# Gated cross-attention and ternary feed-forward block: half the roundings and most of the turns of a unit go from the gate-and-up stage to the down stage, and an input's rounding follows its scale at once

## The reference

```python
def h_bitlinear(x, w):                       # used for gate, up and down
    xq = act_quant(fwht(x))                  # Hadamard transform, then 8 bits per token
    wq = weight_quant(w)                     # ternary weights
    return jnp.einsum('bsh,oh->bso', xq, wq)

x = x + tanh(g_xattn) * attention(layernorm(x), ctx, ctx)        # 32 heads of 16, 8 key heads
gate = h_bitlinear(layernorm(x), w_gate)                         # 512 -> 2048
up   = h_bitlinear(layernorm(x), w_up)
x = x + tanh(g_ffn) * h_bitlinear(silu(gate) * up, w_down)       # 2048 -> 512
```

## Time and profile before

| | us |
|---|---|
| median of 3 runs (lowest, highest) | 530.8 (528.2, 534.39) |
| the profiled execution | 533.5 |
| its span, first to last instruction | 531.6 |

### The profile page before, as it was taken

One profiled execution on the slowest core, in us unless ns is written; L12 is line 12 of the kernel. 1 busy time (PEld: TensorE's weight loads), 2 busy tenths in 40 slices (PEclk: granted clock), 3 DMA queues, 4 the chain that ended last, 5 costly groups with the idle time before them and its releaser, 6 DMA issues.

```text
span 531.6 us, 9904 instructions
## 1 busy us (share of the span) xinstructions
PE 489.0 (92%) x3436; PEld 306.1 (58%) x3436; DVE 401.2 (75%) x772; ACT 320.8 (60%) x504; POOL 215.5 (41%) x313
## 2 busy tenths in 40 slices
PE   3899999989899999869989899989999999989997
PEld 2556666656555444357844458754448864479553
DVE  4768997887666449928988947988965988978791
ACT  3368886777677768757633527643446653388381
POOL 3226456797866441743006634203924200920000
PEclk9999999999899999969999999999999999999999
DMA  7997010010020040000000010000011000000012
GB/s 220 332 353 233 8 34 1 15 28 2 1 80 2 1 160 1 0 1 2 1 1 1 1 59 20 0 0 0 0 39 41 2 0 1 1 1 1 21 60 80
DMA packets 19705, 24.00 MB, mean 45 GB/s; under 512 B 1808, under 2 KB 14480, under 8 KB 19664
## 3 DMA queue, kind: packets, MB, share of 16 engines
q1 hardware_dynamic: 19248, 22.68, 13.4%
q10 hardware_dynamic: 416, 0.79, 0.4%
HBM read 19.26 MB, written 4.19 MB: 44 GB/s over the span
## 4 chain that ended last, share of the span: by engine, by line
PE 62%; issue 17%; DVE 13%; ACT 4%; POOL 2%; DMA 1%; POOLq 1%; SPq 1%; DVEq 0%; ACTq 0%
PE ps L752 9%; PE ps L834 9%; PE ps L535 9%; PE ps L518 7%; PE ps L784 6%; PE ps L561 5%; DVE wst L1345 3%; PE ps L578 3%; DVE wst L1340 2%; DVE reg L1181 2%; PE ps L543 2%; PE ps L681 2%; PE ps L608 2%; ACT y_split L1059 1%; DVE wst L1302 1%
## 5 line engine op out<-in xcount | busy, mean ns | idle before, releaser
L752 PE MATMUL ps<-wst 128*128 128x512 bf16 x512 | 114.2, 379 | 1.5 <-DVE su L1314 1.5
L1181 DVE TENSOR_REDUCE reg<-ps 128x4 f32<-128x512 f32 x128 | 82.0, 685 | 38.3 <-PE ps L535 37.1
L535 PE MATMUL ps<-reg 32*128 32x256 f32 x512 | 91.6, 447 | 1.6 <-DMA reg<-in_k_t 0.9
L488 POOL TENSOR_TENSOR reg_rest<-reg_rest,z_sc 128x1024 f32<-128x1024 f32 x24 | 51.4, 2175 | 90.1 <-DVE z_sc L1383 90.1
L903 ACT ACTIVATE reg<-ps 128x1024 f32<-128x1024 f32 x64 | 65.4, 1022 | 33.6 <-PE ps L543 30.3
L752 PEld LDWEIGHTS ps<-wst 128*128 128x128 bf16 x512 | 48.9, 98 | 58.3 <-DVE su L1314 1.8
L1039 ACT ACTIVATE wst<-wst 128x512 f32<-128x512 f32 x64 | 40.1, 629 | 67.6 <-DVE wst L1340 67.6
L518 PE MATMUL ps<-reg 32*128 32x512 f32 x256 | 76.0, 672 | 0.0
L784 PE MATMUL ps<-had_f,wst 128*128 128x128 f32 x512 | 69.7, 282 | 5.0 <-DVE wst L1345 5.0
L784 PEld LDWEIGHTS ps<-had_f,wst 128*128 128x128 f32 x512 | 66.3, 197 | 8.3 <-DVE wst L1345 5.7
L535 PEld LDWEIGHTS ps<-reg 32*128 32x128 f32 x512 | 62.1, 209 | 7.1 <-ACT reg L925 2.4
(11 more groups left out here) (174 smaller groups left out, 822.4 us busy)
## 6 DMA issues: line engine op xcount, KB each, us to landing
wst<-in_w SPq DMA_DIRECT2D x16, 512.0 KB, 8.8
reg<-in_w SPq DMA_DIRECT2D x8, 512.0 KB, 5.0
out<-x_all SPq DMA_DIRECT2D x16, 256.0 KB, 2.0
x_all<-in_x SPq DMA_DIRECT2D x3, 1024.0 KB, 9.8
reg<-in_k_t SPq DMA_DIRECT2D x32, 32.0 KB, 2.5
reg<-in_v SPq DMA_DIRECT2D x4, 256.0 KB, 3.8
x_all<-in_x ACTq DMA_DIRECT2D x1, 512.0 KB, 4.9
x_all<-in_x ACTq DMA_DIRECT2D x1, 256.0 KB, 3.7
```

The source lines that it names most:

```text
L488: pool.tensor_tensor(z, z, sc, ALU.mult).then_inc(sem("z_scaled"), 1)
L535: last = pe.matmul(ps[:, row_banks(r) + m, 256 * g:256 * g + 256], q_t[n % 4][strip(i), P * h:P * h + P], kpad[n // CHUNK % 2][strip(i), n ...
L752: last = pe.matmul(ps[:, banks[ob % n], :], tern_gu[:, ob // 2, m, j, P * (ob % 2):P * (ob % 2) + P], q1_t[:, j, :], start=(j == 0), stop= ...
L1181: dve.tensor_reduce(neg_max[n % 2][:, g:g + 2, i + m, :], ps[:, row_banks(r) + m, :].rearrange("p (g a t) -> p g a t", g=2, a=2), AX_X, AL ...
```

## The change

In the two passes of the loop DVE rounds pieces 0 to 3 at blocks 11 to 14 (before: pieces 0 to 6 at blocks 9 to 15, and piece 7 behind them). Pieces 4 to 7 are rounded in the down stage, between the statistics and the outputs. PE turns pieces 0 and 1 at blocks 14 and 15 (before: 0 to 3 at blocks 12 to 15), and pieces 2 to 7 in the down stage. ACT makes all eight copies behind its last Silu. Unit 2, whose quantisation runs beside the last gate-and-up stage, keeps the old places. In all three transforms that prepare inputs, the rounding L1302 moves from `input_round` to the end of `input_peak`.

```diff
--- before.py
+++ after.py
@@ -724,7 +724,7 @@
                     if step == SECOND_TURN[tb]:
                         second_turn(batch(u, tb), tb)
 
-            def gate_up(u, chain=None, first=False):
+            def gate_up(u, chain=None, first=False, turns=14):
                 reach(pe, sem("f_q1"), u.times(UB, UB))
                 reach(pe, sem("f_sg"), u.times(UB, UB))
                 if not first:
@@ -752,8 +752,8 @@
                             last = pe.matmul(ps[:, banks[ob % n], :], tern_gu[:, ob // 2, m, j, P * (ob % 2):P * (ob % 2) + P],
                                              q1_t[:, j, :], start=(j == 0), stop=(j == NJ - 1))
                         last.then_inc(sem(name), 1)
-                    if chain is not None and ob >= 12:
-                        turn(chain, ob - 12)
+                    if chain is not None and ob >= turns:
+                        turn(chain, ob - turns)
                     if chain is not None and ob == 2:
                         reach_apart(pe, sem("ones_set"),
                                     (sem("mz_done"), chain.times(8, 8)),
@@ -836,15 +836,17 @@
                 last.then_inc(sem("d_done"), 1)
 
             def project(u):
-                turn(u, 4)
+                turn(u, 2)
                 pe.wait_ge(sem("signed"), 2 * NCH)
                 reach(pe, sem("h_done"), u.times(NC, 2 * NC - 1))
                 down(u, 0, q2_t)
+                turn(u, 3)
+                turn(u, 4)
+                down(u, 1, q2_t)
                 turn(u, 5)
                 turn(u, 6)
-                down(u, 1, q2_t)
+                down(u, 2, q2_t)
                 turn(u, 7)
-                down(u, 2, q2_t)
                 down(u, 3, q2_t)
 
             def project_last(u):
@@ -867,7 +869,7 @@
                 project(Index(i, 0))
             kept_u, last_u = Index(None, NU - 2), Index(None, NU - 1)
             transform(kept_u, last_u)
-            gate_up(last_u, kept_u)
+            gate_up(last_u, kept_u, turns=12)
             pe.wait_ge(sem("h_done"), last_u.times(NC, 14))
             turn_kept(4)
             pe.wait_ge(sem("gs_done"), last_u.times(NC, 15))
@@ -1097,9 +1099,7 @@
                 evacuate(Index(i, 0), Index(i, 1))
                 for ob in range(NC):
                     silu(Index(i, 1), ob)
-                    if ob >= 12:
-                        turned(Index(i, 0), ob - 12, q2_t)
-                for p in range(4, 8):
+                for p in range(8):
                     turned(Index(i, 0), p, q2_t)
                 apply(Index(i, 2), 0)
                 act.wait_ge(sem("d_done"), Index(i, 0).times(UB, UB))
@@ -1295,12 +1295,12 @@
                                   ).then_inc(sem("f_c"), 1)
                 dve.wait_ge(sem("f_c"), n.times(5, 4))
                 dve.tensor_scalar(f_max[:, 3:4], f_max[:, 2:3], QMAX * C_E, None, ALU.mult).then_inc(sem("f_c"), 1)
-
-            def input_round(n, tb, bank=1):
-
                 dve.wait_ge(sem("f_c"), n.times(5, 5))
                 dve.tensor_scalar(q_int, ps[:, bank, :], f_max[:, 3:4], MAGIC, ALU.mult, ALU.add
                                   ).then_inc(sem("f_qf"), 1)
+
+            def input_round(n, tb):
+
                 dve.wait_ge(sem("f_qf"), n.times(1, 1))
                 reach(dve, sem("f_t2"), n.times(1))
                 dve.tensor_scalar(q_b[:, :], q_int, MAGIC, None, ALU.subtract).then_inc(sem("f_qb"), 1)
@@ -1419,7 +1419,7 @@
             for b in range(NB):
                 step(b)
 
-            def gates_and_chain(u, prev):
+            def gates_and_chain(u, prev, first_round=11):
                 reach(dve, sem("a2_done"), u.times(16))
                 for ob in range(NC):
                     gate(u, ob)
@@ -1450,10 +1450,10 @@
                             chain(prev)
                         if ob == 6:
                             chain_end(prev)
-                        if ob >= 9:
-                            rounding(prev, ob - 9)
+                        if ob >= first_round and (first_round < 11 or ob < 15):
+                            rounding(prev, ob - first_round)
                 hidden(u, NC - 1)
-                if prev is not None:
+                if first_round < 11:
                     rounding(prev, 7)
 
             gates_and_chain(Index(None, 0), None)
@@ -1463,15 +1463,23 @@
                 keep_scales(Index(i, 0))
                 split_and_inputs(Index(i, 0), Index(i, 1))
                 gates_and_chain(Index(i, 1), Index(i, 0))
+                rounding(Index(i, 0), 4)
                 front_statistics(Index(i, 2), 0)
                 front_statistics(Index(i, 2), 1)
+                dve.wait_ge(sem("c_f"), Index(i, 0).times(1, 1))
+                output(Index(i, 0), 0)
+                rounding(Index(i, 0), 5)
                 front_statistics(Index(i, 2), 2)
                 front_statistics(Index(i, 2), 3)
-                outputs(Index(i, 0))
+                rounding(Index(i, 0), 6)
+                output(Index(i, 0), 1)
+                rounding(Index(i, 0), 7)
+                output(Index(i, 0), 2)
+                output(Index(i, 0), 3)
             kept_u, u = Index(None, NU - 2), Index(None, NU - 1)
             keep_scales(kept_u)
             split_and_inputs(kept_u, u)
-            gates_and_chain(u, kept_u)
+            gates_and_chain(u, kept_u, 9)
             keep_scales(u)
             for s in range(16):
                 low(u, s)
```

## The result

The changed kernel took 540.6 us (median of 4 runs, 539.25 to 541.88), the kernel before 532.6 beside it (528.2 to 534.58). The ratio is 1.018, with a 95% interval of 1.014 to 1.022: slower by some 8 us of span (539.8 against 531.6), where +4.1 was forecast.

What follows compares the result with a forecast made beforehand. PE was taken to bound everything the change touches. Two passes of 0.7 + 0.9 + 3.0 us cost +9.2, three transforms gain 5.1, so +4.1: 534.9 us against the median of 530.8, range 530.5 to 540.5.

Steps and rivals of the forecast that it cites:

- Part 3: Down stage, each pass: two more turns on PE cost 0.9 us, waits for ACT's copies ahead of downs 1 to 3 cost 3.0.
- Part 2: Start of the down stage: the first down waits for ACT's copy 1 and starts 0.7 us later in each pass.
- Part 1: End of gate and up: with fewer roundings there, DVE reaches gate 15 at 299.9 instead of 301.15, 1.2 us earlier.
- The rival that the clock falls there: Ahead of turn 2: PE's 3.0 us pause halves its clock, some 2 us a pass, +4 in both, 538.9 us; chance 0.17.
- Part 4: Transforms: L1302 no longer stands behind low, so PE's waits go; gain 1.7 us a transform, 5.1 for three.
- The last chain: End of each transform: the chain to the first gate matmul (feed to ACT, su on DVE) moves along.
- What stands behind: Behind the down stage: the next transform's first input turn is just covered, by 0.3 us, although apply begins as down 3 does.

Runs made afterwards that it cites:

- e3: The changed kernel with 13 matmuls of 128x512, result overwritten, put ahead of PE's turn 2 in the loop: 536.4 us, ratio 1.010.
- e9: e4 with the 13 matmuls of e3 ahead of turn 2: 530.3 us against 530.7, ratio 0.998.
- e8: e3 with 4 matmuls instead of 13 ahead of turn 2: 540.9 us, ratio 1.017.
- e2: The changed kernel with the input's rounding put back behind low, so only the move into the down stage: 544.6 us, ratio 1.025.
- e1: The kernel before with only the input's rounding moved behind its scale: 527.2 us against 530.3, ratio 0.992.
- e6: e1 with POOL holding back each unit's third-input butterflies until DVE has made q_b, diag and m8u of the first: 526.3 us, ratio 0.992.
- e4: The changed kernel with turns one group further ahead in the down stage and roundings 4 to 7 ahead of the first output: 534.8 us, ratio 1.008.
- e10: The changed kernel once more, unaltered, beside the kernel before: 540.5 us against 530.7, ratio 1.018.
- e5: e1 with roundings at blocks 9 to 12, 15 and behind the last hidden, all three gate-and-up stages; turns and copies unmoved: 524.3 us, ratio 0.988.

## Why the prediction was wrong

The direction of each part was right and the sum was not: +4.1 forecast, +8.8 in the trace. Of the 4.7 us between them 2.5 are the clock, which the sum had at nothing, 1.2 the transforms and 0.7 the first down. By its steps:

- **Part 3, the down stage: right.** Forecast 0.9 us of turns and 3.0 of waits, 3.9 together. In e3, where the clock stays up, the stage runs from 297.80 to about 316.9, 19.1 us instead of 15.2: 3.9. e9 against e3 takes the waits away, 3.1 us.
- **Part 2, the first down: mis-sized.** Forecast 0.7 us later; in e3 it is 35.35 us behind the first gate matmul, against 34.28 before, 1.07 later. The missing 0.37 is in Part 1: I gave the first rounding 1.1 us from start to start, and it took 1.45 (290.13 to 291.58; the first of the kernel before, at 288.44, had a duration of 1.27 where the others have 1.18). That ACT's copies behind the last Silu hold the first down up is read from the timelines; no run moved only them back.
- **The clock: the step that failed.** The sum took PE's pause ahead of turn 2 as free of any cost beyond its length. The rival that the clock falls there had 0.17 and was put aside because 3.0 us are shorter than 3.33. The pause was 3.3 us, the clock fell to 0.50 behind it in both passes, and e8 shows that 2.46 would have done it too. It cost 1.25 us a pass here (e3), 2.5 in all. The rival's price of 2 us a pass was too high for that, though e2 had 2.3 and 1.2 in its two passes. That its +8.1 lies so near to the measured +8.8 is partly luck: 1.5 too much for the clock stand against 1.9 too little in Parts 2 and 4.
- **Part 4, the input's rounding: right in kind, too large.** Forecast 1.7 us for each transform, measured 1.2, 1.4 and 1.3, and 3.5 for e1 in all. A wait for m8u of 0.3 to 0.4 us stayed. I took q_b and diag for early enough at their new places, though they lie beside POOL's butterflies; e6 shows that these are the cause of the wait: by q_b (0.96) and diag (0.74) in the first transform, by diag alone in the other two. The last chain (su, ACT) is no shorter, as said.
- What stands behind was right: the first input turn of the next transform didn't wait for POOL (322.18 is followed at once), and the four moved roundings took 0.68 us.

Sum with the measured terms: 2 × (3.9 + 1.07 + 1.25) − 3.9 = +8.5, against +8.8. The Trainium skill's warning (TensorE: Matmul & The Clock Gate, section "HAM oscillation — how this bites in real kernels") was the side to take: pauses between bursts bring the half rate back. The traces agree: behind 3.32 or 3.33 us of idle time ahead of turn 2 the clock fell to 0.50 in both passes of four traces (the changed kernel, e2, e4, e10), and behind 2.46 us in both passes of e8.

## What to carry to other kernels

Moving work off the engine that a stage waits for pays only if what depends on that work keeps its distance: moving roundings alone (e5) was worth 2.2 us, and when turns and copies went with them, the waits alone lost 3.0 us a pass, because a copy that had a whole down to hide in now stood right ahead of its reader. (Two more turns in the down stage were 0.9 on top.) Ask of a moved producer where its consumer is, and leave one unit of the consumer's work between them. And count a pause that the new order opens on TensorE at more than its length: the ones of 2.46 to 3.33 us here cost 1.2 to 2.3 us more behind them.

## What the runs showed of the hardware

DVE's TENSOR_SCALAR from SBUF to SBUF took about half the time, or less, when POOL was quiet. 128x1024 to bf16: 0.68 us alone, 1.18 to 1.52 beside POOL; 128x512 to bf16: 0.41 against up to 0.96; 128x128 in float32: 0.28 against 0.74. For the last two e6 shows POOL as the cause; for the first it is read from where POOL's scaling ends. The Trainium skill (GPSIMD Engine Reference, section "1. Specifications") says that POOL shares its SBUF interfaces with VectorE, with contention for DVE instructions in a 2-port mode or with two SBUF inputs. The traces agree that DVE is slower beside POOL; in which mode these operations ran they don't say. A wait of 0.3 to 0.4 us on TensorE disappeared when POOL, which had time to spare, was made to wait.

Neither the fall of the clock nor its length is fixed by the pause: behind the same 3.3 us it cost 1.25 us in one kernel, 1.4 in another execution of it, and 2.3 and 1.2 in the two passes of e2. Behind a pause of 1.70 us the clock stayed at 1.00 in the last unit of the kernel before and of e1, and fell in e6. What decides that was not tried.
